# Sixteen-head attention: values and sums gathered by one matmul, divided by token, turned back

## The reference

```python
def attention(query, key, value, mask, Wq, bq, Wk, bk, Wv, bv, Wo, bo):
    q, k, v = split_heads(query @ Wq + bq), split_heads(key @ Wk + bk), split_heads(value @ Wv + bv)
    scores = jnp.einsum('bhqd,bhkd->bhqk', q, k) / np.sqrt(8)
    scores = masked(scores, mask)            # layer 2: mask[q, k]; layer 3: a mask over the keys
    probs = jax.nn.softmax(scores, axis=-1)
    attn = jnp.einsum('bhqk,bhkd->bhqd', probs, v)
    return attn.transpose(0, 2, 1, 3).reshape(B, -1, 128) @ Wo + bo

x = x + jnp.tanh(g_xattn[n]) * attention(layernorm(x), ctx, ctx, mask, ...)
x = x + jnp.tanh(g_ffn[n]) * feed_forward(layernorm(x), ...)
```

## Time and profile before

| | |
|---|---|
| time, median of 3 runs | 1187.66 us (1187.41 to 1188.54) |
| profiled execution, its own time | 1187.89 us |
| its span, first to last instruction | 1186.2 us |
| TensorE busy | 1104.4 us (93%) |
| VectorE busy | 738.9 us (62%) |
| ScalarE busy | 695.6 us (59%) |
| GpSimd busy | 468.8 us (40%) |
| mean granted TensorE clock | 0.976 of full speed |
| a2, first to last reduction | 693.35 to 793.87 us |
| a3, first to last reduction | 878.11 to 977.73 us |

### The profile page before, as it was taken

The page is one execution under the profiler, slowest core; times in us unless marked ns, Lnnn a source line. Parts: engine busy times, 40 slices in busy tenths (PEclk is TensorE's granted clock), DMA queues, the critical chain, the costliest instruction groups (busy, mean ns, idle before and its releaser), DMA issues. The chain is left out here.

```text
span 1186.2 us, 24457 instructions
## 1 busy us (share of the span) xinstructions
PE 1104.4 (93%) x9849; PEld 808.2 (68%) x9865; DVE 738.9 (62%) x1385; ACT 695.6 (59%) x1226; POOL 468.8 (40%) x737
## 2 busy tenths in 40 slices
PE   5987898899999999999998989998979998999998
PEld 3553368788888888888887556763647764466667
DVE  6762457555665566665664269995659995645554
ACT  4675530466666656666666567777447877644440
POOL 5771001223323323444434354431573534645441
PEclk9898899899999999999999899999989999999999
DMA  9200000100000000000000200000000000033320
GB/s 340 85 2 1 0 1 2 71 2 1 2 2 1 1 2 1 1 2 1 2 1 1 54 1 2 2 3 1 1 1 2 2 2 2 9 96 102 98 76 18
DMA packets 13889, 29.52 MB, mean 25 GB/s; under 512 B 2737, under 2 KB 5073, under 8 KB 13010
## 3 DMA queue, kind: packets, MB, share of 16 engines
q1 hardware_dynamic: 13778, 27.96, 7.1%
HBM read 25.14 MB, written 1.25 MB: 22 GB/s over the span
## 5 line engine op out<-in xcount | busy, mean ns | idle before, releaser
L1252 POOL TENSOR_TENSOR work<-work 128x1024 f32<-128x1024 f32 x64 | 121.3, 1896 | 268.1 <-DVE work L1346 268.1
L1333 DVE TENSOR_REDUCE work<-psum 128x8 f32<-128x1024 f32 x64 | 78.0, 1219 | 86.1 <-PE psum L1132 86.1
L1274 ACT ACTIVATE work<-work 128x1024 f32<-128x1024 f32 x64 | 67.4, 1053 | 95.8 <-DVE work L1337 95.8
L1344 DVE TENSOR_REDUCE work<-work 128x8 f32<-128x1024 f32 x64 | 77.4, 1209 | 72.1 <-ACT work L1274 72.1
L1703 PEld LDWEIGHTS psum<-w_down,work 128*128 128x128 f32 x768 | 99.1, 192 | 27.1 <-issue 25.6
L1703 PE MATMUL psum<-w_down,work 128*128 128x128 f32 x768 | 100.2, 275 | 1.1 <-DVE x L1823 0.7
L991 ACT ACTIVATE work<-psum 128x512 f32<-128x512 f32 x128 | 73.0, 596 | 37.7 <-PE psum L858 36.7
L858 PEld LDWEIGHTS psum<-ident,work 128*128 128x128 f32 x512 | 57.7, 143 | 44.0 <-ACT work L988 24.6
L1031 DVE TENSOR_REDUCE work<-psum 128x8 f32<-128x1024 f32 x64 | 75.2, 1216 | 14.4 <-PE psum L844 14.1
L858 PE MATMUL psum<-ident,work 128*128 128x128 f32 x512 | 76.4, 283 | 6.9 <-ACT work L991 5.6
L1337 DVE TENSOR_TENSOR work<-psum,work 128x1024 f32<-128x1024 f32 x64 | 78.4, 1225 | 6.4
(11 more groups left out here) (339 smaller groups left out, 2534.9 us busy)
## 6 DMA issues: line engine op xcount, KB each, us to landing
work<-chosen SPq DMA_DIRECT2D x80, 128.0 KB, 2.9
x<-in_x SPq DMA_DIRECT2D x2, 512.0 KB, 4.9
ctx_tok<-in_ctx SPq DMA_DIRECT2D x2, 512.0 KB, 6.8
xnt<-in_xt SPq DMA_DIRECT2D x1, 1024.0 KB, 9.2
ctxt<-in_ctxt SPq DMA_DIRECT2D x1, 1024.0 KB, 11.1
mask<-in_mask SPq DMA_DIRECT2D x1, 1024.0 KB, 9.9
w_down<-in_down SPq DMA_DIRECT2D x1, 1024.0 KB, 8.3
ctx_tok<-in_g SPq DMA_DIRECT2D x1, 1024.0 KB, 4.7
```

Source lines behind the costliest of these rows:

```text
L1252: pool.tensor_tensor(prob[:, u % 2, h, :], prob[:, u % 2, h, :], rinv[:, u % 2, h].unsqueeze(2).broadcast_to([P, 8, P]), ALU.mult)\
L1274: act.activation(p, p, ACT.Exp).then_inc(S["exp"], 1)
L1333: dve.tensor_reduce(nmax[:, u % 2, h], s, AX.X, ALU.max, negate=True).then_inc(S["max"], 1)
L1344: dve.tensor_reduce(rsum[:, u % 2, h], prob[:, u % 2, h, :], AX.X, ALU.add).then_inc(S["sum"], 1)
```

## The change

The values `vp` get a column block of ones beside each head's eight columns, so that one column-tiled matmul a head gives eight rows of values and eight of its sum. Groups g = 0 and 1 share a 128-column part of bank 6, and 2 and 3 the next; an odd group's weights are read from 16 columns earlier, so that its rows lie at 16 to 31 of the 32. The matmuls with `ones8` are gone. ScalarE copies the gathered 128x256 to SBUF (`keep_gathered`); two transposes turn it to tokens in bank 7, columns 256 to 511 (`turn_to_tokens`); VectorE takes the reciprocals of sixteen columns of sums and multiplies the sixteen heads' eight columns by them (`divided`, 128x128); one transpose turns this back into bank 6, columns 256 to 383 (`turn_back`); ScalarE copies it to `ot` (`keep_back`). The output matmul, the residual and the normalised tail come one block later than before, and the steps after the loop are rewritten. `wo`'s rows are laid out for the new order of heads on the host.

```diff
@@ -776,24 +776,27 @@
     nc, bank, psum = k.nc, k.bank, k.psum
     a = Arena(k)
     qt = a.take(2 * GT, "p (n c) -> p n c", n=2)
     kt = a.take(2 * GT, "p (n c) -> p n c", n=2)
     vr = a.take(2 * GT, "p (n c) -> p n c", n=2)
     km = a.take(2 * 512, "p (n i c) -> p n i c", n=2, i=4)
-    vp = a.take(2 * 544, "p (n c) -> p n c", n=2)
+    vp = a.take(2 * 576, "p (n c) -> p n c", n=2)
     prob = a.take(2 * T, "p (n c) -> p n c", n=2)
     probt = a.take(4 * 512, "p (n c) -> p n c", n=4)
     nmax = a.take(2 * 16, "p (n h) -> p n h", n=2)
-    rinv = a.take(P)
+    rinv = a.take(16)
+    gathered = a.take(2 * 256, "p (n c) -> p n c", n=2)
+    divided = a.take(2 * P, "p (n s c) -> p n s c", n=2, c=8)
     ot = a.take(2 * P, "p (n c) -> p n c", n=2)
     bn = a.take(6)
     wq, wk, wv, wo = (k.w[n] for n in names)
     scale = 8.0 ** -0.5
     S = {n: k.sem(f"{tag}_" + n) for n in
          (*(("rotated",) if turn_mask else ()), "setup", "stepped", "zero", "proj", "k", "q", "v", "km", "vp", "score", "max", "sub", "exp", "turn", "pt", "pv",
-          "inv", "on", "out", "added", "stated", "xb", "sel", "chain", "root", "normed", "turned", "kept")}
+          "ones", "kept_pv", "token", "inv", "on", "back", "ot", "out", "added", "stated", "xb", "sel", "chain", "root", "normed", "turned", "kept")}
     after = NormalisedTail(k, a, S, lambda n: bank[4], 2)
     def fills(b):
@@ -804,10 +807,16 @@
     def filled(b):
         return 3 + sum(fills(n) is not None for n in range(b))
-    def scatter(t):
-        return t.rearrange("p (g r) -> p g r", r=136)[:, :, 0:128]\
-                .rearrange("p g (i c) -> p g i c", c=32)[:, :, :, 0:8]
+    def slots(t, at):
+        return t.rearrange("p (g r) -> p g r", r=144)[:, :, 0:128]\
+                .rearrange("p g (i c) -> p g i c", c=32)[:, :, :, at:at + 8]
+    def columns(b, g, i):
+        at = 144 * g - 16 * (g % 2) + 32 * i
+        return vp[:, b % 2, at:at + 32]
+    by_token = bank[7][:, 256:512]
     def tensor(pe):
         def project(g, which, out):
@@ -849,8 +858,8 @@
             n = 4 * b + g
             if g % 2 == 0:
                 pe.wait_ge(S["exp"], 2 * b + g // 2 + 1)
-            if g == 0 and b >= 6 and b % 2 == 0:
-                pe.wait_ge(S["kept"], (b - 6) // 2 + 1)
+            if g == 0 and b >= 7 and b % 2 == 1:
+                pe.wait_ge(S["kept"], (b - 7) // 2 + 1)
             if n >= 2:
                 pe.wait_ge(S["pt"], n - 1)
             for i in range(4):
@@ -861,28 +870,44 @@
         def gather(b):
             pe.wait_ge(S["vp"], b + 1)
-            if b:
-                pe.wait_ge(S["on"], b)
+            if b >= 1:
+                pe.wait_ge(S["kept_pv"], b)
+            if b >= 2:
+                pe.wait_ge(S["ot"], b - 1)
             for g in range(4):
                 pe.wait_ge(S["pt"], 4 * b + g + 1)
                 for i in range(4):
-                    r, h = slice(32 * i, 32 * i + 32), 4 * g + i
-                    pe.matmul(bank[6][r, 0:P], vp[:, b % 2, h * 32:(h + 1) * 32],
-                              probt[:, g, i * P:(i + 1) * P],
-                              start=(g == 0), stop=False, skip_group_check=True)
-                for i in range(4):
-                    r = slice(32 * i, 32 * i + 32)
-                    mm = pe.matmul(bank[6][r, P:2 * P], k.ones8[:, g, :],
-                                   probt[:, g, i * P:(i + 1) * P],
-                                   start=False, stop=(g == 3), skip_group_check=True)
+                    mm = pe.matmul(bank[6][32 * i:32 * i + 32, g // 2 * P:(g // 2 + 1) * P], columns(b, g, i),
+                                   probt[:, g, i * P:(i + 1) * P], start=g == 0, stop=g % 2 == 1,
+                                   skip_group_check=True)
             mm.then_inc(S["pv"], 1)
-        def out(b, fills_before):
+        def settled(fills_before):
+            pe.wait_ge(S["v"] if fills_before % 3 == 0 else S["k"] if fills_before % 3 == 1 else S["q"],
+                       -(-fills_before // 3))
+        def turn_to_tokens(b):
+            pe.wait_ge(S["kept_pv"], b + 1)
+            if b:
+                pe.wait_ge(S["on"], b)
+            for half in range(2):
+                mm = pe.transpose(by_token[:, half * P:(half + 1) * P], gathered[:, b % 2, half * P:(half + 1) * P],
+                                  k.ident[:, :])
+            mm.then_inc(S["token"], 1)
+        def turn_back(b):
             pe.wait_ge(S["on"], b + 1)
+            pe.wait_ge(S["kept_pv"], min(NB, b + 2))
+            if b:
+                pe.wait_ge(S["ot"], b)
+            pe.transpose(bank[6][:, 256:256 + P], divided[:, b % 2, :, :].rearrange("p s c -> p (s c)"), k.ident[:, :])\
+              .then_inc(S["back"], 1)
+        def out(b):
+            pe.wait_ge(S["ot"], b + 1)
             if b:
                 pe.wait_ge(S["added"], b)
-            pe.wait_ge(S["v"] if fills_before % 3 == 0 else S["k"] if fills_before % 3 == 1 else S["q"],
-                       -(-fills_before // 3))
             pe.matmul(bank[7][:, 0:P], ot[:, b % 2, :], wo[:, :], start=True, stop=True)\
               .then_inc(S["out"], 1)
@@ -900,9 +925,11 @@
                 score(b)
             if b:
                 turn(b - 1, 0)
+                if b >= 3:
+                    turn_back(b - 3)
                 if at := fills(b):
                     if b >= 3:
-                        pe.wait_ge(S["added"], b - 2)
+                        pe.wait_ge(S["on"], b - 2)
                     elif b == 1:
                         prev.ready(pe, NG - 1)
                     if at[1] > 0:
@@ -911,14 +938,23 @@
                 turn(b - 1, 1)
                 turn(b - 1, 2)
                 if b >= 2:
-                    out(b - 2, filled(b + 1))
+                    settled(filled(b + 1))
+                if b >= 3:
+                    out(b - 3)
+                if b >= 2:
+                    turn_to_tokens(b - 2)
                 turn(b - 1, 3)
-                if b >= 6 and b % 2 == 0:
+                if b >= 7 and b % 2 == 1:
                     pe.wait_ge(S["pt"], 4 * b - 1)
-                    after.turn(pe, (b - 6) // 2)
+                    after.turn(pe, (b - 7) // 2)
                 gather(b - 1)
+        turn_back(NB - 2)
+        out(NB - 2)
+        turn_to_tokens(NB - 1)
+        after.turn(pe, NB // 2 - 3)
+        turn_back(NB - 1)
+        out(NB - 1)
         after.turn(pe, NB // 2 - 2)
-        out(NB - 1, filled(NB))
         yield
         after.turn(pe, NB // 2 - 1)
@@ -938,6 +974,9 @@
         keys(0)
         yield
         pool.memset(vp[:, :, :], 0.0).then_inc(S["zero"], 1)
+        pool.wait_ge(S["zero"], 1)
+        for n in range(2):
+            pool.memset(slots(vp[:, n, :], 8), 1.0).then_inc(S["ones"], 1)
         for b in range(NB + 1):
             if 0 < b < NB:
                 keys(b)
@@ -945,12 +984,10 @@
                 m = b - 1
                 if m % GB == 0:
                     pool.wait_ge(S["v"], m // GB + 1)
-                if m == 0:
-                    pool.wait_ge(S["zero"], 1)
                 if m >= 2:
                     pool.wait_ge(S["pv"], m - 1)
                 src = vr[:, (m // GB) % 2, (m % GB) * P:(m % GB + 1) * P]
-                pool.tensor_tensor(scatter(vp[:, m % 2, :]),
+                pool.tensor_tensor(slots(vp[:, m % 2, :], 0),
                                    src.rearrange("p (g i c) -> p g i c", g=4, i=4),
                                    bv.rearrange("p (g i c) -> p g i c", g=4, i=4),
                                    ALU.add).then_inc(S["vp"], 1)
@@ -960,8 +997,9 @@
                 xg = xv[:, b * GB:(b + 1) * GB, :]
                 pool.tensor_tensor(xg, xg, bo.unsqueeze(1).broadcast_to([P, GB, P]), ALU.add)\
                     .then_inc(S["xb"], 1)
-            if b >= 4 and b % 2 == 0:
-                after.root(pool, (b - 4) // 2)
+            if b >= 5 and b % 2 == 1:
+                after.root(pool, (b - 5) // 2)
+        after.root(pool, NB // 2 - 2)
         yield
         after.root(pool, NB // 2 - 1)
@@ -979,21 +1017,45 @@
             act.wait_ge(S["proj"], n + 1)
             evict(0, n, src)
         yield
+        def exponential(b, half):
+            act.wait_ge(S["sub"], 2 * b + half + 1)
+            p = prob[:, b % 2, half * 1024:(half + 1) * 1024]
+            act.activation(p, p, ACT.Exp).then_inc(S["exp"], 1)
+        def keep_gathered(b):
+            act.wait_ge(S["pv"], b + 1)
+            if b >= 2:
+                act.wait_ge(S["token"], b - 1)
+            act.activation(gathered[:, b % 2, :], bank[6][:, 0:256], ACT.Copy).then_inc(S["kept_pv"], 1)
+        def keep_back(b):
+            act.wait_ge(S["back"], b + 1)
+            if b >= 2:
+                act.wait_ge(S["out"], b - 1)
+            act.activation(ot[:, b % 2, :], bank[6][:, 256:256 + P], ACT.Copy).then_inc(S["ot"], 1)
         for b in range(NB):
-            if b >= 5 and b % 2 == 1:
```

(43 more changed lines are left out.)

## The result

The changed kernel takes 1185.43 us (median of 12 runs, 1182.01 to 1187.45) against 1188.1 (12 runs, 1184.0 to 1191.67): ratio 0.9975, interval 0.9963 to 0.9987. That is about 3 us, faster: the interval is clear of no change, and its middle is just over the 0.2% that I had set as the bound of a measurable change, though its end of 0.13% is under it. I had forecast no change, so the forecast was wrong, though the time lies in the range.

The account below looks back on a forecast made before the run. VectorE and TensorE, both full, were taken to bound the kernel, with the score loop under both. 1187.9 - 8.2 (loops and starts) + 6.6 (ends) + 2.0 (clock) = 1188.3 us, no measurable change; range 1182.5 to 1193.5.

Parts of the forecast that it names:

- a score loop under both: Scores, reductions and subtractions share four banks: no block shorter than 6.2 us in the second attention, 6.0 in the third.
- VectorE's part: VectorE's block in the attention loop: narrower reciprocal, 0.25 instead of 0.93 us, takes it from 6.49 to 5.8.
- rival (d): Strided reciprocal stays at 0.93 us, VectorE's block at 6.5, ending as (c); chance 0.10 together with (c).
- ScalarE's: ScalarE in the attention loop: two more evictions a block, 0.65 us, raise it from 75 to 78% busy to about 88%.
- the two new waits: VectorE's residual awaits the transposes to tokens, the transpose back awaits VectorE's product: both cost nothing in the loop.
- the chain of hand-overs at the ends: After each attention's last reduction: next stage's first matmul at 15.1 us instead of 11.79, 3.3 later, twice: +6.6.
- TensorE's part: TensorE's block: 0.88 us less gathering, three added transposes at 0.53 with gaps; net -0.35, ends -0.55 and -0.03.
- rival (a): Faster: added transposes cost 0.33 us without gaps and the clock holds, 1183; chance with its side 0.33.
- The late exponential: ScalarE's first exponential delays TensorE's next transposes in two blocks of the third attention; 0.25 us charged there.
- The clock: TensorE's granted clock may fall in the lull after each attention: one fall of 2.0 us charged for both ends, 0 to 7.
- (c): Loop period doesn't fall since ScalarE holds TensorE's transposes; only starts gain, ends cost: 1195; chance 0.10 together with rival (d).
- The starts: First blocks of both attentions: -0.85 and -0.95 us without the new transposes, 0.5 given back by memsets.

Follow-up runs that it names:

- runs 1 and 2: Kernel before with, in turn, only the reciprocal narrowed to 128x16 (ratio 0.9981), and only 12 of 16 matmuls of sums a block left out (0.9979).
- run 3: Kernel before with both the reciprocal narrowed to 128x16 and 12 of 16 matmuls of sums a block left out: 1172.87 us, ratio 0.9879.
- Run 6: Changed kernel with another order after the loop alone, block 15's operations ahead of block 14's, tail's transposes behind the next stage's first matmuls: 1180.11 us, ratio 0.9924.
- runs 7 and 8: Kernel before with two unread transposes more a block, ahead of the last group of transposes (ratio 0.9998), or between that group and the gather (1.0015).
- Run 4: Changed kernel with two unread float32 matmuls of 512 columns where TensorE waits in the last steps of each attention: 1182.99 us, ratio 0.9966.

## Why the prediction was wrong

What it said of the bounds was right: two engines nearly tied and a score loop under both at 6.2 and 6.0 us (measured 6.22 and 5.98, in the third attention with VectorE 0.1 us behind); relief of one alone gives little (runs 1 and 2), both together go to the loop (run 3). Right too were VectorE's part (0.23 us for the reciprocal, so rival (d) is out), ScalarE's (85% busy where I wrote about 88), the two new waits, which cost nothing in the loop, and the chain of hand-overs at the ends: 15.1 us, +3.3 an end, measured 15.08 and 15.09. Run 6 shows that it was this order. That the two agree to the hundredth is luck: counted from reduction 15 (790.17), block 15's reciprocal starts at 12.2 and the last output matmul at 13.7 where I had 12.65 and 14.0, and the low clock, which I charged apart, then stretches that matmul and the tail's transposes.

**The step that failed is TensorE's part, the price of the added transposes.** I read the gaps of its queue (0.46 on the chain for an output matmul whose two passes take 0.22) as what a short operation behind waits costs, and charged the three new transposes 0.33 of streaming and 0.20 of gaps: net -0.35 a block. They were waits for ScalarE, which the view of waits books as "issue" or, being short, does not list. This is the timeline of before: the block of the earlier trace rows, and the two ends of the next block's way from its first group of transposes to its gather:

```profile
755.51 0.69 ACT L971 ACTIVATE work<-psum,cols 128x512 f32<-128x512 f32 x1 [0.26 <-PE psum L816]
...
756.10 1.08 ACT L991 ACTIVATE work<-psum 128x512 f32<-128x512 f32 x2
...
756.35 0.46 PE L886 MATMUL psum<-w_wo,work 128*128 128x128 f32 x2
...
756.74 0.66 PE L858 MATMUL psum<-ident,work 128*128 128x128 f32 x4
...
760.65 0.66 PE L858 MATMUL psum<-ident,work 128*128 128x128 f32 x4
...
764.29 0.43 PE L870 MATMUL psum<-work 128*32 128x128 f32 x8
```

The output matmul starts 0.15 after the projection's eviction (755.51, 0.69 long) has ended, which it awaits because both use bank 7; the last group of transposes starts at 756.74, right after ScalarE's copy of the second group, the first of the two from 756.10 (0.60 long), has freed their bank. After the change, the same places of one block:

```profile
765.15 0.66 PE L867 MATMUL psum<-ident,work 128*128 128x128 f32 x4
...
766.85 0.60 ACT L1014 ACTIVATE work<-psum 128x512 f32<-128x512 f32 x1 [0.16 <-PE psum L831]
767.34 1.08 ACT L1046 ACTIVATE work<-psum 128x512 f32<-128x512 f32 x2
...
767.52 0.47 PE L911 MATMUL psum<-w_wo,work 128*128 128x128 f32 x2
...
767.83 0.38 PE L895 MATMUL psum<-ident,work 128*128 128x128 f32 x2
...
768.04 0.60 PE L867 MATMUL psum<-ident,work 128*128 128x128 f32 x4
...
768.85 1.08 PE L880 MATMUL psum<-work 128*32 128x128 f32 x32
```

The new pair (L895, 767.83) sits in that second wait: the last group starts 0.10 after the copy begun at 767.34 has ended, where before it started 0.04 after. Such a pair costs up to 0.07 there and 0.13 to 0.26 behind that group (runs 7 and 8). In a block with a projection and the tail's pair, TensorE goes from its first transposes to its gather in 3.64 us before (760.65 to 764.29) and in 3.70 after (765.15 to 768.85), three transposes of 0.11 more in it. The fullest block, 6.96 us in the second attention before, fits into 6.22 afterwards: with 0.88 less gathering, the three added transposes cost it at most 0.14 us instead of 0.53. To take away the gaps alone, as rival (a) did, is not enough: at 0.33 the sum would still have had this block at 6.42. So no block is TensorE's any more, the eight projection blocks of each attention reach the loop too, and the gain in the loops was 11.9 us instead of the 6.9 of my sums. The lower end that I had given, "-0.55", was no bound either, since it allowed the streaming nothing to hide in. The late exponential that I charged 0.25 for in the third attention does not show. A smaller slip: I took 6.69 for every projection block of the second attention and 6.96 with the tail's pair, which before the change only blocks 2 and 10 have (table of runs 7 and 8).

**The clock was mis-sized in the other direction.** I charged one fall of 2.0 for two ends; in the profiled execution it fell at both, for 2.2 each, 4.4. Run 4 shows the cause: with the lull filled, both stretches are back to 6.28 and 7.05. The Trainium skill, page "TensorE: Matmul & The Clock Gate" (Part 1: The HAM clock gate), says that the slow clock is the default and that activity releases it. With my price of 2 for a fall, that rule gave about 4 us for both ends; this trace agrees, with 4.4.

The sum: gains of 13.8 instead of 8.2, ends of 11.0 instead of 8.6. The two errors, 5.6 and 2.4, had opposite signs, so that the time came within 3 us of the forecast is in part luck; what was left, 3 us, is just over the bound. Rival (a) named the right side with the wrong limits: it had the transposes without gaps, but 3 us for it, and the clock held. Of (c) nothing came true.

The starts gave 0.58 and 1.33, 1.9 in all where I had 1.3. The third attention's start varies by itself: run 4, whose loop starts as the changed kernel's does, has 14.65 for it, and run 6 has 13.86. So up to 0.8 of the 13.8 is not the change's.

## What to carry to other kernels

A gap in TensorE's queue that the profile books as "issue", or doesn't list, may be a wait for an eviction: look up what ended just before it on the engine that frees the bank. Here work put into such a gap cost a third of its length or less, and the same work next to it all of it, so price an insertion by its place, not by the kind. The further stage of this software pipeline cost next to nothing in the loop and was paid in full where the pipeline drains: follow the last block through every queue, and let its operations go first; here that order alone was worth another 5 to 6 us, about twice the change.

## What the runs showed of the hardware that I had not expected

Between the end of block 15's gather (799.40) and the next stage's first gate matmul (805.25) TensorE had only single transposes, pairs of them and two output matmuls to do. The granted clock fell in the stretch from 802 to 804, and the fall cost 2.2 us of the following stage at each of the two ends; two unread matmuls of 1.13 and 1.02 us in the lull kept it at 1.00. With the shorter lull of run 6 it held 1.00 for that stage's first matmuls, yet was 0.50 behind them, from 810 to 812; why it fell there and not in run 4, which idles as much in that place (0.46 busy in 808 to 810, granted clock 1.00), stays open.

Twelve executions of one and the same kernel lie between 1184.0 and 1191.67 us, though its thirteen blocks repeat to 0.04 us from profile to profile (80.86, 80.82 and 80.85 in the changed kernel and runs 4 and 6). For a change inside such a stretch two traces show what the ratio of times can tell only from many executions; for what hangs on the clock, one trace is one case.
